# Cross-attention in a decoder layer: key-pair sums on GpSimd, normalisation on ScalarE, the sums' matmuls moved into the middle of a step

## The chip, the cores and the metric

The kernel runs on one core of one Trainium2 chip. The metric is the device time of one execution in microseconds (us); lower is better. The times come from separate timed executions. The profile is one further execution, recorded by the hardware profiler. Engines: PE is TensorE (PEld its weight loads), DVE is VectorE, ACT is ScalarE, POOL is GpSimd, SP is the engine whose queue issues the DMAs.

## What is computed

Inputs are x and ctx, both 16 x 256 x 512 in float32. Three blocks follow one another, each added to x:

```python
x = x + self_attention(layernorm(x))                 # 16 heads, causal, rotary
x = x + cross_attention(layernorm(x), ctx, ctx, gamma)
x = x + expert_mix(layernorm(x))                     # router, top-k tokens per expert

def cross_attention(q, k, v, gamma):                 # all (16, 256, 512)
    h = 8
    qh = q.reshape(16, h, 256 // h, 512)             # heads split the 256 rows: 32 rows each
    kh, vh = (t.reshape(16, h, 256 // h, 512) for t in (k, v))
    qk = einsum('bhdq,bhdl->bhql', qh, kh) / sqrt(32)
    ret = einsum('bhql,bhdl->bhdq', softmax(qk, -1), vh)
    return gamma * ret.reshape(16, 256, 512)
```

So in the cross-attention the contraction runs over 32 rows, and queries and keys are the 512 columns. Only this block is changed.

## The kernel before

The blocks run one after another, with all engines meeting between them: layer norm 1 (to 106 us), self-attention (to about 2014 us), cross-attention (about 2017 to 2704 us), expert mix (the rest).

**Tiles and steps.** The cross-attention has 32 tiles of 128 rows, and a tile holds 4 heads of 32 rows. A tile has 4 steps, one for each chunk `c` of 128 keys, so there are 128 steps `s = 4n + c`. "Step 0" to "step 3" of a tile below mean `c`. In a step PE does, for each of the 4 heads, one `scores` matmul (L774) for the tile that is six steps ahead (AHEAD = 6) and one `transposed_scores` matmul (L783) for this step. After the second head it does the `middle` of the step. At the step's end it does `weigh` (L794, values times weights) and `sums` (L804, a column of ones times weights) for the step before. `weigh` and `sums` are 4 fp32 matmuls each on 32-column strips of the array, shown as 8 instructions each.

**Two passes over the scores.** `scores` exist only to find the maximum of each query: DVE reduces each bank (L941, `xnmx`). A tile's 16 maxima are transposed by PE (`max_transposes`, L819, middle of step 2 for tile n+1), rounded by ACT (`max_round`, L902, `xmhi`), the rest of the rounding is taken by DVE (`max_rest`, L946, `xmlo`), and the two parts are written by DMA as two more rows of the stacked queries (`max_rows`, L736). `transposed_scores` then give scores less maximum, and ACT takes the exponential from PSUM into `xprt` (L878). Scores use two PSUM banks (`xsc`), transposed scores two (`xst`).

**Preparing a tile.** `load` (L711, L712) brings x and ctx, DVE normalises (`normed`, L932, `xn`), ACT rounds to the PE's fast format (`q_round` L867, `k_round` L872), POOL takes the rest (`split`, L752 and L755). The parts are written to DRAM (`write_parts`, L716 and L718) and read back in six DMAs into three sets of stacks of 96 rows (`read_stacks`, L729 and L730). All DMAs are issued by SP, in this order, each `wait_ge` holding up all that is behind it:

```python
for n in range(-4, TILES):
    if tile(n + 2): read_stacks(n + 2)   # waits until both write_parts(n + 2) have landed
    if tile(n + 1): max_rows(n + 1)      # waits for xmhi, then for xmlo
    if tile(n + 3): write_parts(n + 3)
    if tile(n + 4): load(n + 4)
```

The first `scores` that need the stacks of tile n+2 are those of step 4n+2, that is of step 2 of tile n.

**Finishing a tile.** ACT moves the sums out (`sums_evac`, L896), PE brings them to queries on partitions (`sums_by_query`, L826), DVE inverts them (`one_over_sums`, L952), ACT repeats each 32 times (`repeat`, L907), PE transposes back (`inverses`, L834), DVE multiplies (`output`, L956) and adds gamma times the result to x (`residual`, L960), and takes the statistics for the next layer norm (L965, L969). The tables `WORK` say behind which head of which step ACT and DVE do these things, and for which tile.

Of the kernel before, what the change touches and what calls it, by code (L numbers as in the profile page):

```python
# [625 lines left out]
def cross_attention(nc, x1, ctx_in, gamma, sq, sk, mv2, mv3, x2, cst):  # L626
# [4 lines left out]
    with ctx:  # L631
# [16 lines left out]
        gam = sb("gam", [P, 1], F32)  # L648
        tmp = sb("rs_tmp2", [P, 2, TILES], F32)
        rstd = sb("rstd2", [P, TILES], F32)  # L650
        cin = sb("cin", [P, 4, D], F32)
        xn = sb("xn2", [P, D], F32)
        qp = sb("qp", [P, 2, D], F32R)
# [19 lines left out]
        SU = pb("xsu")  # L673
        VB = pb("xvb")

        s_gam, s_var, s_sqrt, s_step = sem("x_gam"), sem("x_var"), sem("x_sqrt"), sem("x_step")
        s_xi = [sem(f"x_xi{i}") for i in range(4)]
        s_ci = [sem(f"x_ci{i}") for i in range(4)]
# [7 lines left out]
        s_mt, s_mhi, s_mlo = sem("x_mt"), sem("x_mhi"), sem("x_mlo")  # L686
        s_vt, s_vte = sem("x_vt"), sem("x_vte")
        s_ts, s_exp = sem("x_ts"), sem("x_exp")
        s_pv, s_su = sem("x_pv"), sem("x_su")
        s_oe, s_se = sem("x_oe"), sem("x_se")  # L690
        s_sq, s_ri, s_rr, s_rt = sem("x_sq"), sem("x_ri"), sem("x_rr"), sem("x_rt")
        s_on, s_x2, s_bn = sem("x_on"), sem("x_x2"), sem("x_bn")
# [2 lines left out]
        cv = ctx_in.rearrange("b (t p) d -> (b t) p d", p=P)  # L695
        x1v = x1.rearrange("b p t d -> b t p d")

        FIRST, LAST = -4 * CB, CB * (TILES + 2)

        def tile(n):  # L700
            return 0 <= n < TILES
# [1 line left out]
        @block.sync  # L703
        def _(sp):
            sp.dma_start(gam[:, :], gamma.rearrange("(a b) -> a b", a=1).broadcast_to([P, 1])).then_inc(s_gam, 16)

            def load(m):
                if m >= 4:
                    sp.wait_ge(s_vt, m - 3)
                    sp.wait_ge(s_klo, m - 3)  # L710
                sp.dma_start(x2[:, m, :], x1v[m // 2, m % 2]).then_inc(s_xi[m % 4], 16)  # L711
                sp.dma_start(cin[:, m % 4, :], cv[m]).then_inc(s_ci[m % 4], 16)  # L712

            def write_parts(m):
                sp.wait_ge(s_qlo, m + 1)
                sp.dma_start(sq[m % 2].rearrange("h p d -> p h d"), qp[:, :, :].bitcast(F32)).then_inc(s_qw, 16)  # L716
                sp.wait_ge(s_klo, m + 1)
                sp.dma_start(sk[m % 2].rearrange("h p d -> p h d"), kp[:, :, :].bitcast(F32)).then_inc(s_kw, 16)  # L718

            def read_stacks(m):  # L720
                sp.wait_ge(s_qw, 16 * m + 16)
                sp.wait_ge(s_kw, 16 * m + 16)
                if m >= STACKS:
                    sp.wait_ge(s_ts, 16 * (m - STACKS) + 16)
                qv = sq[m % 2].rearrange("h (j r) d -> h r j d", j=XPT)
                kv = sk[m % 2].rearrange("h (j r) d -> h r j d", j=XPT)
                for c in range(PARTS):
                    rows = slice(XD * c, XD * (c + 1))
                    sp.dma_start(qst[m % STACKS][rows, :, :].bitcast(F32), qv[c // 2]).then_inc(s_st[m % STACKS], 16)  # L729
                    sp.dma_start(kst[m % STACKS][rows, :, :].bitcast(F32), kv[c % 2]).then_inc(s_st[m % STACKS], 16)  # L730

            def max_rows(m):
                for k, (part, here) in enumerate(((mhi, s_mhi), (mlo, s_mlo))):
                    sp.wait_ge(here, m + 1)
                    row = qst[m % STACKS][KS + k:KS + k + 1, :, :].rearrange("o h (q n) -> o (h q) n", n=P)
                    sp.dma_start(row.bitcast(F32), part[:, :].bitcast(F32)).then_inc(s_row[m % STACKS], 16)  # L736

            for n in range(-4, TILES):
                if tile(n + 2):
                    read_stacks(n + 2)  # L740
                if tile(n + 1):
                    max_rows(n + 1)
                if tile(n + 3):
                    write_parts(n + 3)
                if tile(n + 4):
                    load(n + 4)

        @block.gpsimd
        def _(pool):
            def split(m):  # L750
                pool.wait_ge(s_qhi, m + 1)
                nc.gpsimd.tensor_tensor(qp[:, 1, :], xn[:, :], qp[:, 0, :].bitcast(F32),  # L752
                                        ALU.subtract).then_inc(s_qlo, 1)
                pool.wait_ge(s_khi, m + 1)
                nc.gpsimd.tensor_tensor(kp[:, 1, :], cin[:, m % 4, :], kp[:, 0, :].bitcast(F32),  # L755
                                        ALU.subtract).then_inc(s_klo, 1)

            for i in range(STACKS):
                nc.gpsimd.memset(kst[i][KS:KM, :, :].bitcast(F32), 1.0).then_inc(s_ones, 1)
                pool.wait_ge(s_ones, i + 1)  # L760
            nc.gpsimd.memset(ones[:, :], 1.0).then_inc(s_ones, 1)
            for n in range(-3, TILES + 1):
                if tile(n + 3):
                    split(n + 3)

        @block.tensor
        def _(pe):
# [27 lines left out]
                                            start=(c == 0), stop=(c == CB - 1))  # L795
                last.then_inc(s_pv, 1)

            def sums(s):
                n, c = s // CB, s % CB
                if c == 0:  # L800
                    pe.wait_ge(s_se, n)
                for h in range(XPT):
                    rows = slice(XD * h, XD * (h + 1))
                    last = nc.tensor.matmul(SU[rows, :], ones[:, :], prt[s % RING][:, h, :],  # L804
                                            start=(c == 0), stop=(c == CB - 1))
                last.then_inc(s_su, 1)

            def values(n):
# [26 lines left out]
                last.then_inc(s_rt, 1)  # L835

            def middle(n, c):
                if c == 0 and tile(n):
                    values(n)
                if c == 1 and tile(n - 2):  # L840
                    inverses(n - 2)
                if c == 2 and tile(n + 1):
                    max_transposes(n + 1)
                if c == 3 and tile(n - 1):
                    sums_by_query(n - 1)

            pe.wait_ge(s_ones, STACKS + 1)
            for s in range(FIRST, LAST):
                for i in range(XPT):
                    if 0 <= s + AHEAD < STEPS:  # L850
                        scores(s + AHEAD, i)
                    if 0 <= s < STEPS:
                        transposed_scores(s, i)
                    if i == 1:
                        middle(s // CB, s % CB)
                if 0 <= s - 1 < STEPS:
                    weigh(s - 1)
                    sums(s - 1)

        @block.scalar  # L860
        def _(act):
            rstd_of_all(nc, act, None, rstd, tmp, s_var, s_sqrt, s_step, scale=XSCALE)

            def q_round(m):
                act.wait_ge(s_qn, m + 1)
# [8 lines left out]
            def exps(s, h):  # L874
                act.wait_ge(s_ts, 4 * s + h + 1)
                if h == 0 and s >= RING:
                    act.wait_ge(s_su, s - RING + 1)
                nc.scalar.activation(prt[s % RING][:, h, :], ST[h % 2][:, :], ACT.Exp).then_inc(s_exp, 1)  # L878

            def v_evac(n):  # L880
# [10 lines left out]
                nc.scalar.activation(osb[n % 2][:, :], OB[:, :], ACT.Copy).then_inc(s_oe, 1)  # L891

            def sums_evac(n):
                act.wait_ge(s_su, CB * n + CB)
                act.wait_ge(s_sq, n)
                nc.scalar.activation(ssb[:, :], SU[:, :], ACT.Copy).then_inc(s_se, 1)  # L896

# [6 lines left out]
            def repeat(n):  # L904
                act.wait_ge(s_ri, n + 1)
                act.wait_ge(s_rt, n)
                nc.scalar.activation(rrep[:, :, :].rearrange("p q (h r) -> p (q h) r", r=XD),  # L907
                                     rq[:, :].unsqueeze(2).broadcast_to([P, CB * XPT, XD]), ACT.Copy).then_inc(s_rr, 1)

            WORK = {(0, 1): ((repeat, -2),), (0, 2): ((v_evac, 0),), (1, 0): ((output_evac, -1), (sums_evac, -1)),  # L910
                    (1, 2): ((q_round, 3),), (1, 3): ((k_round, 3),), (2, 2): ((max_round, 1),)}

            for s in range(FIRST, LAST):
                n, c = s // CB, s % CB
# [8 lines left out]
        def _(dve):  # L923
            nc.vector.tensor_scalar(tmp[:, 0, :], mv2[:, :, 1], EPS, None, ALU.add).then_inc(s_var, 1)
            dve.wait_ge(s_var, 1)
            rstd_of_all(nc, None, dve, rstd[:, :], tmp, s_var, s_sqrt, s_step, scale=XSCALE)
            dve.wait_ge(s_gam, 16)

            def normed(m):
                dve.wait_ge(s_xi[m % 4], 16 * (m // 4 + 1))  # L930
                dve.wait_ge(s_qlo, m)
                nc.vector.tensor_scalar(xn[:, :], x2[:, m, :], mv2[:, m, 0:1], rstd[:, m:m + 1],  # L932
                                        ALU.subtract, ALU.mult).then_inc(s_qn, 1)

            def maximum(g, q):
                m, h = g // CB, g % CB
# [16 lines left out]

            def output(n):
                dve.wait_ge(s_rt, n + 1)
                nc.vector.tensor_tensor(onm[:, :], osb[n % 2][:, :], VB[:, :], ALU.mult).then_inc(s_on, 1)  # L956

            def residual(n):
                dve.wait_ge(s_on, n + 1)
                nc.vector.scalar_tensor_tensor(x2[:, n, :], onm[:, :], gam[:, 0:1], x2[:, n, :], ALU.mult,  # L960
                                               ALU.add).then_inc(s_x2, 1)

            def statistics(n):
                dve.wait_ge(s_x2, n + 1)
                nc.vector.bn_stats(bn[:, :], x2[:, n, :]).then_inc(s_bn, 1)  # L965

            def mean_and_variance(n):
                dve.wait_ge(s_bn, 2 * n + 1)
                nc.vector.bn_aggr(mv3[:, n, :], bn[:, :]).then_inc(s_bn, 1)  # L969

            WORK = {(0, 0): ((normed, 3),), (2, 0): ((output, -2),), (2, 1): ((residual, -2),), (2, 2): ((max_rest, 1),),
                    (3, 0): ((statistics, -2),), (3, 1): ((mean_and_variance, -2),), (3, 3): ((one_over_sums, -1),)}

            for s in range(FIRST, LAST):
                n, c = s // CB, s % CB
# [410 lines left out]
```

## Time and profile before

| | before |
|---|---|
| median of 3 timed runs | 3007.75 us (3007.65 to 3009.14) |
| the profiled execution, its own time | 3004.79 us |
| its span in the trace | 3002.7 us |
| PE busy over the span | 2765.7 us (92%) |
| PEld | 2064.0 us (69%) |
| DVE | 1828.5 us (61%) |
| ACT | 1010.2 us (34%) |
| POOL | 589.9 us (20%) |
| mean granted PE clock | 0.962 |

The times of views are from the span's start. "Busy" of an engine is the time in which it has an instruction under way; matmuls are pipelined, so a busy PE need not be at its peak. In the cross-attention the page's slices show PE at 9 tenths, ACT at 5, DVE at 6, POOL at 1 and the DMA engines at 5 to 6. In rows of the order of time, a row is: start, duration, engine, line, operation, out<-in, shapes, count, and in brackets how long the engine was idle before it and what ended that. "issue" means that nothing in the profile was waited for. SPq rows are DMAs being issued by SP. The granted clock of 1.00 is 2.4 GHz, 0.50 is 1.2 GHz.

### The profile page before, as it was taken

The page shows a single profiled execution, that of the slowest core. Times are in us where ns is not written, and L with a number is a line of the kernel's source. Part 1 is how long each engine was busy: PE and PEld are TensorE (multiplying, and loading weights), DVE is VectorE, ACT ScalarE, POOL GpSimd, SP SyncE. Part 2 cuts the span into 40 slices and gives each one's busy share as a digit, 9 for nine tenths or more (in the row PEclk, how much of TensorE's full clock was granted, in tenths as well). Part 3 has the DMA queues.
Part 4 walks back from the last instruction along what each step waited for, and adds up shares of the span by engine and source line. Part 5 has one row for each costly group of instructions (what it writes and reads, how often), then busy time and mean ns, then how long its engine had stood idle before and what let it go on. Part 6 is the DMA issues. An engine that isn't in the chain of part 4 may idle for free. (4 is left out here: it accounts for less than half of the span.)

```text
span 3002.7 us, 40644 instructions
## 1 busy us (share of the span) xinstructions
PE 2765.7 (92%) x14237; PEld 2064.0 (69%) x14238; DVE 1828.5 (61%) x3578; ACT 1010.2 (34%) x2511; POOL 589.9 (20%) x498
## 2 busy tenths in 40 slices
PE   3799999999999999999999999977999999997973
PEld 2588888888888888888888888863444444447852
DVE  7465556566656665565656566655666666643488
ACT  2222222322222332222322222223555555553321
POOL 2121112321211321111322111211111111100263
PEclk9999999999999999999999999997999999995697
DMA  8421122222211421221222112117666556610003
GB/s 315 154 84 57 57 92 92 85 71 99 71 57 57 154 71 57 73 96 57 92 90 101 57 57 99 43 55 186 152 164 166 155 149 165 164 42 18 0 0 112
DMA packets 165203, 290.02 MB, mean 97 GB/s; under 512 B 11680, under 2 KB 78240, under 8 KB 162976
## 3 DMA queue, kind: packets, MB, share of 16 engines
q1 hardware_dynamic: 165024, 287.66, 30.9%
q8 instruction: 110, 1.80, 0.3%
q14 instruction: 69, 0.57, 0.1%
HBM read 194.81 MB, written 92.27 MB: 96 GB/s over the span
## 5 line engine op out<-in xcount | busy, mean ns | idle before, releaser
L439 PE MATMUL pj<-xnt,whi 128*128 128x512 f32 x2048 | 704.1, 405 | 16.1 <-DMA xnt<-xt_scratch 16.1
L519 ACT ACTIVATE pr<-sc,nmx 128x128 f32<-128x128 f32 (+1 forms) x512 | 210.6, 416 | 934.0 <-DVE nmx L591 934.0
L941 DVE TENSOR_REDUCE xnmx<-xsc 128x1 f32<-128x512 f32 x512 | 338.6, 683 | 231.2 <-PE xsc L774 228.2
L439 PEld LDWEIGHTS pj<-xnt,whi 128*128 128x128 f32 x2048 | 385.6, 188 | 108.3 <-DMA xnt<-xt_scratch 16.5
L439 PE MATMUL pj<-xnt,wlo 128*128 128x512 f32 x1024 | 398.6, 389 | 0.0
L394 POOL TENSOR_TENSOR qt<-rot,swp 128x512 f32<-128x512 f32 x128 | 166.0, 1297 | 1126.4 <-DVE swp L572 1126.4
L878 ACT ACTIVATE xprt<-xst 128x512 f32<-128x512 f32 x512 | 294.0, 603 | 264.2 <-PE xst L783 262.4
L436 PE MATMUL pj<-whi,xnt 128*128 128x512 f32 x1024 | 351.7, 405 | 0.0
L570 DVE TENSOR_TENSOR rot<-pj,trig 128x512 f32<-128x512 f32 x256 | 176.8, 691 | 226.6 <-PE pj L439 226.6
L774 PE MATMUL xsc<-kst,qst 96*128 96x512 f32 x512 | 245.1, 483 | 52.5 <-DMA kst<-sk_scratch 29.9
L591 DVE TENSOR_REDUCE nmx<-sc 128x1 f32<-128x128 f32 (+1 forms) x512 | 158.3, 351 | 177.4 <-PE sc L465 172.8
L600 DVE TENSOR_SCALAR pr<-pr,rinv 128x128 f32<-128x128 f32 (+1 forms) x512 | 251.8, 533 | 9.0
L774 PEld LDWEIGHTS xsc<-kst,qst 96*128 96x128 f32 x512 | 98.8, 193 | 224.5 <-DVE xnmx L941 111.5
L436 PEld LDWEIGHTS pj<-whi,xnt 128*128 128x128 f32 x1024 | 192.5, 188 | 45.9
L783 PE MATMUL xst<-qst,kst 98*128 98x512 f32 x512 | 207.6, 408 | 17.1 <-ACT xprt L878 17.1
L394 POOL TENSOR_TENSOR kt<-rot,swp 128x512 f32<-128x512 f32 x128 | 165.0, 1289 | 296.4 <-DVE swp L572 296.4
L439 PEld LDWEIGHTS pj<-xnt,wlo 128*128 128x128 f32 x1024 | 193.9, 189 | 34.5
L452 PE MATMUL pj<-whi,ohi 128*128 128x512 f32 x512 | 212.5, 415 | 1.4 <-DVE olo L605 1.4
L579 DVE TENSOR_TENSOR xio<-pj,xio 128x512 f32<-128x512 f32 x128 | 88.5, 691 | 192.3 <-PE pj L452 192.3
L452 PE MATMUL pj<-whi,olo 128*128 128x512 f32 x512 | 201.6, 394 | 0.0
L452 PE MATMUL pj<-wlo,ohi 128*128 128x512 f32 x512 | 199.1, 389 | 0.0
L436 PE MATMUL pj<-wlo,xnt 128*128 128x512 f32 x512 | 199.1, 389 | 0.0
(152 smaller groups left out, 4483.4 us busy)
## 6 DMA issues: line engine op xcount, KB each, us to landing
xnt<-xt_scratch SPq DMA_DIRECT2D x64, 1024.0 KB, 8.0
x_scratch<-xio SPq DMA_DIRECT2D x64, 512.0 KB, 3.6
xio<-x_scratch SPq DMA_DIRECT2D x48, 512.0 KB, 4.1
qst<-sq_scratch SPq DMA_DIRECT2D x96, 256.0 KB, 5.6
kst<-sk_scratch SPq DMA_DIRECT2D x96, 256.0 KB, 6.2
xt_scratch<-parts SPq DMA_DIRECT2D x16, 1024.0 KB, 4.7
sq_scratch<-qp SPq DMA_DIRECT2D x32, 512.0 KB, 3.0
sk_scratch<-kp SPq DMA_DIRECT2D x32, 512.0 KB, 4.1
```

Of the source, the lines that this page charges most:

```text
L394: nc.gpsimd.tensor_tensor(qk["QK".index(kind)][h][:, :, :].rearrange("p b n -> p (b n)"), rot[r % 2][:, :], swp[r % 2][:, :], ALU.add).the ...
L436: last = nc.tensor.matmul(bank[:, :], moving[:, i * P:(i + 1) * P], wpart[:, w, :], start=(k == 0), stop=(k == 3 * CB - 1))
L439: last = nc.tensor.matmul(bank[:, :], wpart[:, w, i * HD:(i + 1) * HD], moving, start=(k == 0), stop=(k == 3 * CB - 1))
L452: last = nc.tensor.matmul(PJ[n % 3][:, :], o[:, h, tok], w[:, CH_O + h, :], start=(h == 0 and k == 0), stop=(h == HG - 1 and k == 2))
L519: nc.scalar.activation(pr[:, a % 4, lo:hi], SC[a % 2][:, lo:hi], ACT.Exp, bias=nmx[:, a % 4, t:t + 1], accum_out=rsum[:, a % 4, t:t + 1]). ...
L570: nc.vector.tensor_tensor(ro, bank, table(slice(0, P), q), ALU.mult)
L591: nc.vector.tensor_reduce(nmx[:, a % 4, t:t + 1], SC[a % 2][:, lo:hi], AX.X, ALU.max, negate=True).then_inc(s_nmx, 1)
L600: nc.vector.tensor_scalar(pr[:, a % 4, lo:hi], pr[:, a % 4, lo:hi], rinv[:, a % 4, t:t + 1], None, ALU.mult).then_inc(s_pr, 1)
L774: nc.tensor.matmul(SC[q % 2][:, :], qst[m % STACKS][0:KS, h, q * P:(q + 1) * P], kst[m % STACKS][0:KS, h, :], start=True, stop=True).then_ ...
L783: nc.tensor.matmul(ST[h % 2][:, :], kst[n % STACKS][0:KM, h, c * P:(c + 1) * P], qst[n % STACKS][0:KM, h, :], start=True, stop=True).then_ ...
L878: nc.scalar.activation(prt[s % RING][:, h, :], ST[h % 2][:, :], ACT.Exp).then_inc(s_exp, 1)
L941: nc.vector.tensor_reduce(nmx[:, m % 2, k:k + 1], SC[q % 2][:, :], AX.X, ALU.max, negate=True).then_inc(s_mx, 1)
```

## The change

- **Pair sums on POOL.** For each pair of neighbouring steps POOL adds the weights of the second to those of the first, in place, in 4 pieces of 128x512 (`pair_sum`). PE then multiplies by ones only once for a pair: 2 groups of `sums` in a tile in place of 4.
- **Where the sums' groups are.** They are no longer at a step's end but in its middle: for tile n-1, in steps 0 and 2, before the values' transposes and before the maxima's transposes.
- **Normalisation on ACT.** `normed` leaves DVE (step 0, head 0) and is one activation on ACT (step 0, head 3) with scale `rstd` and bias `shift` = -mean x rstd, which one new DVE instruction makes for all tiles.
- **Residual on POOL.** gamma is multiplied in `repeat`; the addition to x is a 128x512 addition on POOL. The statistics on DVE follow one tile later (steps 0 of tile n for tile n-3).
- **ACT's order.** `sums_evac` moves from step 1, head 0 to step 2, head 3; `q_round` and `k_round` one head earlier.
- **SP's order.** The first four `load`s are issued ahead of everything; in the steady loop the order is as it was. The loops of the steps run 3 steps longer.

```diff
-        FIRST, LAST = -4 * CB, CB * (TILES + 2)
+        FIRST, LAST = -4 * CB, CB * (TILES + 2) + 3
@@ block.sync
-            for n in range(-4, TILES):
+            for m in range(4):
+                load(m)
+            for n in range(-3, TILES):
...
-                if tile(n + 4):
+                if n >= 0 and tile(n + 4):
                     load(n + 4)
@@ block.gpsimd
+            def pair_sum(n, k):
+                s = CB * n + 2 * k
+                a, b = prt[s % RING], prt[(s + 1) % RING]
+                pool.wait_ge(s_pv, s + 1)
+                for h in range(XPT):
+                    pool.wait_ge(s_exp, 4 * (s + 1) + h + 1)
+                    nc.gpsimd.tensor_tensor(a[:, h, :], a[:, h, :], b[:, h, :], ALU.add).then_inc(s_add, 1)
+
+            def residual(n):
+                pool.wait_ge(s_on, n + 1)
+                nc.gpsimd.tensor_tensor(x2[:, n, :], onm[:, :], x2[:, n, :], ALU.add).then_inc(s_x2, 1)
...
-            for n in range(-3, TILES + 1):
+            for n in range(-3, TILES + 2):
+                if tile(n - 1):
+                    pair_sum(n - 1, 1)
                 if tile(n + 3):
                     split(n + 3)
+                if tile(n):
+                    pair_sum(n, 0)
+                if tile(n - 2):
+                    residual(n - 2)
@@ block.tensor
-            def sums(s):
-                n, c = s // CB, s % CB
-                if c == 0:
+            def sums(n, k):
+                pe.wait_ge(s_add, XPT * (2 * n + k + 1))
+                if k == 0:
                     pe.wait_ge(s_se, n)
...
             def middle(n, c):
-                if c == 0 and tile(n):
-                    values(n)
+                if c == 0:
+                    if tile(n - 1):
+                        sums(n - 1, 0)
+                    if tile(n):
+                        values(n)
                 if c == 1 and tile(n - 2):
                     inverses(n - 2)
-                if c == 2 and tile(n + 1):
-                    max_transposes(n + 1)
+                if c == 2:
+                    if tile(n - 1):
+                        sums(n - 1, 1)
+                    if tile(n + 1):
+                        max_transposes(n + 1)
...
                     weigh(s - 1)
-                    sums(s - 1)
@@ block.scalar
+            def normed(m):
+                act.wait_ge(s_xi[m % 4], 16 * (m // 4 + 1))
+                act.wait_ge(s_qlo, m)
+                nc.scalar.activation(xn[:, :], x2[:, m, :], ACT.Identity, scale=rstd[:, m:m + 1],
+                                     bias=shift[:, m:m + 1]).then_inc(s_qn, 1)
...
-            WORK = {(0, 1): ((repeat, -2),), (0, 2): ((v_evac, 0),), (1, 0): ((output_evac, -1), (sums_evac, -1)),
-                    (1, 2): ((q_round, 3),), (1, 3): ((k_round, 3),), (2, 2): ((max_round, 1),)}
+            WORK = {(0, 1): ((repeat, -2),), (0, 2): ((v_evac, 0),), (0, 3): ((normed, 3),), (1, 0): ((output_evac, -1),), (1, 1): ((q_round, 3),),
+                    (1, 2): ((k_round, 3),), (2, 2): ((max_round, 1),), (2, 3): ((sums_evac, -1),)}
@@ block.vector
-            WORK = {(0, 0): ((normed, 3),), (2, 0): ((output, -2),), (2, 1): ((residual, -2),), (2, 2): ((max_rest, 1),),
-                    (3, 0): ((statistics, -2),), (3, 1): ((mean_and_variance, -2),), (3, 3): ((one_over_sums, -1),)}
+            WORK = {(0, 1): ((statistics, -3),), (0, 2): ((mean_and_variance, -3),), (2, 0): ((output, -2),),
+                    (2, 2): ((max_rest, 1),), (3, 3): ((one_over_sums, -1),)}
```

The exponentials' wait for a free buffer of the ring of 5 changes with it: a buffer that was added to waits for the pair's `sums`, one that was added from for POOL's additions.

## Rows read from the trace of the kernel before

**Rows 1.** Order of time, PE's weight loads: one tile's step starts and step ends.

```profile
2300.61 0.19 PEld L774 LDWEIGHTS xsc<-kst,qst 96*128 96x128 f32 x1 [0.84 <-issue]
...
2303.60 0.16 PEld L794 LDWEIGHTS xob<-xprt,vt 128*32 128x32 f32 x8 [0.36 <-ACT xprt L878]
2304.06 0.13 PEld L804 LDWEIGHTS xsu<-xprt,xones 128*32 128x32 f32 x4 [0.30 <-issue]
2304.49 0.13 PEld L804 LDWEIGHTS xsu<-xprt,xones 128*32 128x32 f32 x4 [0.30 <-issue]
2305.46 0.19 PEld L774 LDWEIGHTS xsc<-kst,qst 96*128 96x128 f32 x1 [0.84 <-issue]
...
2308.35 0.19 PEld L783 LDWEIGHTS xst<-qst,kst 98*128 98x128 f32 x1 [0.82 <-ACT xprt L878]
...
2310.74 0.19 PEld L774 LDWEIGHTS xsc<-kst,qst 96*128 96x128 f32 x1 [0.94 <-DMA kst<-sk_scratch]
...
2313.22 0.19 PEld L774 LDWEIGHTS xsc<-kst,qst 96*128 96x128 f32 x1 [0.86 <-DVE xnmx L941]
...
2315.74 0.19 PEld L774 LDWEIGHTS xsc<-kst,qst 96*128 96x128 f32 x1 [0.84 <-DVE xnmx L941]
...
2320.73 0.19 PEld L774 LDWEIGHTS xsc<-kst,qst 96*128 96x128 f32 x1 [0.84 <-issue]
```

**Rows 2.** Waits, SP's own, 2100 to 2650 us: total us, times, longest.

```profile
SPq L736 <- ACT xmhi L902: 279.3, 27, 10.9
SPq L724 <- DMA sk_scratch<-kp: 47.3, 28, 3.3
```

**Rows 3.** Order of time, step 2 of the tile of rows 1, then SP's queue.

```profile
2312.02 0.50 PE L774 MATMUL xsc<-kst,qst 96*128 96x512 f32 x1
...
2312.80 0.60 ACT L878 ACTIVATE xprt<-xst 128x512 f32<-128x512 f32 x1 [0.20 <-PE xst L783]
...
2313.29 0.25 ACT L902 ACTIVATE xmhi<-xmx 16x128 fp32r<-16x128 f32 x1
...
2314.34 0.27 DVE L946 TENSOR_TENSOR xmlo<-xmx,xmhi 16x128 fp32r<-16x128 f32 x1
...
2314.64 0.51 SPq L736 DMA_DIRECT2D qst<-xmlo  x1
...
2322.59 0.43 SPq L730 DMA_DIRECT2D kst<-sk_scratch  x1
```

**Rows 4.** Issue to landing of the one kst read issued at 2322.59.

```profile
DMA to landing us min/median/max: 7.1/7.1/7.1
```

**Rows 5.** Order of time, first and last step 2 that wait for a read of stacks.

```profile
2070.63 0.50 PE L774 MATMUL xsc<-kst,qst 96*128 96x512 f32 x1 [2.02 <-DMA kst<-sk_scratch]
...
2650.78 0.19 PEld L774 LDWEIGHTS xsc<-kst,qst 96*128 96x128 f32 x1 [0.84 <-DMA kst<-sk_scratch]
```

**Rows 6.** Groups by line, 2050 to 2750 us: the costs of a POOL piece and of DVE's residual.

```profile
L755 POOL TENSOR_TENSOR kp<-cin,kp 128x512 fp32r<-128x512 f32 x30 | 38.5, 1285 | 0.0
...
L960 DVE SCALAR_TENSOR_TENSOR x<-xonm,gam,x 128x512 f32<-128x512 f32 x32 | 23.8, 743 | 0.1
```

**Rows 7.** Order of time: ctx's second load at the start, the block's last instruction.

```profile
2027.09 0.95 SPq L712 DMA_DIRECT2D cin<-in_ctx_in_dram  x1
...
2704.15 0.18 DVE L969 BATCH_NORM_AGGREGATE mv<-bn 128x2 f32<-128x6 f32 x1
```

**Rows 8.** Busy time and granted clock (third last column), after the stall before 2070.63.

```profile
2072.00:2073.00 1.00, 1.00 (x4) 0.54 (x4) 1.00 (x2) 0.81 (x2) 0.00 (x0) 0.87 0.00 0
...
2075.00:2076.00 1.00, 1.00 (x8) 0.20 (x4) 0.00 (x0) 0.00 (x0) 0.00 (x0) 0.50 0.15 53
2076.00:2077.00 1.00, 1.00 (x10) 0.32 (x3) 0.00 (x0) 0.00 (x0) 0.00 (x0) 0.92 1.01 379
```

**Rows 9.** Order of time, a stall in the self-attention.

```profile
1520.73 0.67 PE L484 MATMUL ob<-prt,v 128*128 128x256 f32 x2 [2.06 <-DVE olo L605]
```

**Rows 10.** Busy time and granted clock behind the stall of rows 9.

```profile
1522.00:1524.00 2.00, 2.00 (x10) 1.61 (x9) 1.92 (x5) 0.45 (x2) 0.80 (x1) 1.00 0.88 315
```

More of the change, by code:

```diff
@@ L650, in cross_attention @@
         rstd = sb("rstd2", [P, TILES], F32)
+        shift = sb("shift2", [P, TILES], F32)
         cin = sb("cin", [P, 4, D], F32)
@@ L674, in cross_attention @@
         VB = pb("xvb")
+        s_shift = sem("x_shift")
         s_gam, s_var, s_sqrt, s_step = sem("x_gam"), sem("x_var"), sem("x_sqrt"), sem("x_step")
@@ L688, in cross_attention @@
         s_ts, s_exp = sem("x_ts"), sem("x_exp")
-        s_pv, s_su = sem("x_pv"), sem("x_su")
+        s_pv, s_add, s_su = sem("x_pv"), sem("x_add"), sem("x_su")
         s_oe, s_se = sem("x_oe"), sem("x_se")
@@ L803, in sums @@
                     rows = slice(XD * h, XD * (h + 1))
-                    last = nc.tensor.matmul(SU[rows, :], ones[:, :], prt[s % RING][:, h, :],
-                                            start=(c == 0), stop=(c == CB - 1))
+                    last = nc.tensor.matmul(SU[rows, :], ones[:, :], prt[(CB * n + 2 * k) % RING][:, h, :],
+                                            start=(k == 0), stop=(k == 1))
                 last.then_inc(s_su, 1)
@@ L862, in _ @@
             rstd_of_all(nc, act, None, rstd, tmp, s_var, s_sqrt, s_step, scale=XSCALE)
+            act.wait_ge(s_gam, 16)
+            act.wait_ge(s_shift, 1)
+            def normed(m):
[3 more added lines that the diff above has]
+                                     bias=shift[:, m:m + 1]).then_inc(s_qn, 1)
             def q_round(m):
@@ L876, in exps @@
                 if h == 0 and s >= RING:
-                    act.wait_ge(s_su, s - RING + 1)
+                    old = s - RING
+                    act.wait_ge(s_pv, old + 1)
+                    if old % 2 == 0:
+                        act.wait_ge(s_su, old // 2 + 1)
+                    else:
+                        act.wait_ge(s_add, XPT * (old // 2 + 1))
                 nc.scalar.activation(prt[s % RING][:, h, :], ST[h % 2][:, :], ACT.Exp).then_inc(s_exp, 1)
@@ L893, in sums_evac @@
             def sums_evac(n):
-                act.wait_ge(s_su, CB * n + CB)
+                act.wait_ge(s_su, 2 * n + 2)
                 act.wait_ge(s_sq, n)
@@ L907, in repeat @@
                 nc.scalar.activation(rrep[:, :, :].rearrange("p q (h r) -> p (q h) r", r=XD),
-                                     rq[:, :].unsqueeze(2).broadcast_to([P, CB * XPT, XD]), ACT.Copy).then_inc(s_rr, 1)
-            WORK = {(0, 1): ((repeat, -2),), (0, 2): ((v_evac, 0),), (1, 0): ((output_evac, -1), (sums_evac, -1)),
-                    (1, 2): ((q_round, 3),), (1, 3): ((k_round, 3),), (2, 2): ((max_round, 1),)}
+                                     rq[:, :].unsqueeze(2).broadcast_to([P, CB * XPT, XD]), ACT.Copy,
+                                     scale=gam[:, 0:1]).then_inc(s_rr, 1)
+            WORK = {(0, 1): ((repeat, -2),), (0, 2): ((v_evac, 0),), (0, 3): ((normed, 3),), (1, 0): ((output_evac, -1),), (1, 1): ((q_round, 3),),
+                    (1, 2): ((k_round, 3),), (2, 2): ((max_round, 1),), (2, 3): ((sums_evac, -1),)}
             for s in range(FIRST, LAST):
@@ L926, in _ @@
             rstd_of_all(nc, None, dve, rstd[:, :], tmp, s_var, s_sqrt, s_step, scale=XSCALE)
[L927 to L933, printed above, removed]
+            nc.vector.scalar_tensor_tensor(shift[:, :], mv2[:, :, 0], -1.0, rstd[:, :], ALU.mult, ALU.mult).then_inc(s_shift, 1)
             def maximum(g, q):
@@ L955, in output @@
                 dve.wait_ge(s_rt, n + 1)
+                dve.wait_ge(s_x2, n)
                 nc.vector.tensor_tensor(onm[:, :], osb[n % 2][:, :], VB[:, :], ALU.mult).then_inc(s_on, 1)
[L958 to L961, printed above, removed]
             def statistics(n):
                 dve.wait_ge(s_x2, n + 1)
+                dve.wait_ge(s_bn, 2 * n)
                 nc.vector.bn_stats(bn[:, :], x2[:, n, :]).then_inc(s_bn, 1)
```

## Prediction

> **What bounds the kernel now.** I read the order of time of PE's weight loads first, to cut a tile into its four steps. A tile takes 20.1 us [rows 1]: steps of 4.85, 5.28, 5.00 and 4.99 us. A step ends with `weigh` and `sums`, together 1.86 us (2303.60 to 2305.46), of which a group of `sums` is two passes 0.43 us apart, 0.87 us. What the change takes away thus stands on PE's path, and PE looks like the bound. The reader should then look at the start of step 2. At 2310.74 the weight load was ended by a DMA, the last read of the key stacks, with 0.94 us of idle time where 0.84 us is what such a load always shows. So PE and the DMAs are within 0.1 us of one another there.
>
> The second view is SP's own waits. SP waited 279 us in 27 tiles, some 10 us a tile, for `xmhi` [rows 2]. All that SP does behind that wait is late with it: the row of `xmlo`, then both `write_parts`, two loads, then `read_stacks`, which also waits until the writes have landed (47 us in 28 tiles). The reads land for PE's step 2, and `xmhi` is made from transposes in PE's step 2. That closes a ring, one turn per tile, and PE's other work isn't in it:
>
> scores of step 2 start, maxima transposed, rounded, rest taken, row of `xmlo` issued, parts written, stacks read, scores of the next tile's step 2.
>
> Its length [rows 3, 4]: from 2310.74 to the issue of `xmlo`'s row at 2314.64 is 3.90 us; from there to the last issue of a read, 2322.59, 7.95 us; to its landing 7.1 us. The queue's part is 15.05 us in that tile. Over the 30 tiles whose reads are waited for it is 14.7 to 16.2 us, mean 15.44. The ring is 3.90 + 15.44 + 0.03 = 19.4 us on average, and up to 20.1 us. The tile's mean is (2650.78 - 2070.63) / 29 = 20.0 us [rows 5]. So PE's path is the longer, by 0.6 us on average, and in the tiles with late reads by nothing. **Whatever is taken off PE's path beyond 0.6 us a tile is not gained unless the ring gets shorter too.**
>
> **The change, part by part.** *PE's own path.* Two groups of `sums` fewer: 2 x 0.87 = 1.7 us. A group in the middle of a step has to drain and refill the array beside full-height matmuls; no row shows that. Bounds: 0.87 us, as at the step's end, and 1.2 us (the 0.87 with one more wait of 0.30 us as in rows 1); I take 1.05, nearer to what the end of a step shows with its neighbours. In step 1 the wait of 0.82 us for ACT (2308.35) goes, since `sums_evac` leaves that place; in step 2 most of the 0.86 us for DVE (2313.22) goes, with `residual`. New steps: 4.85 - 0.87 + 1.05 - 0.3 = 4.7; 5.28 - 0.87 - 0.6 = 3.8; 5.00 - 0.87 + 1.05 - 0.7 = 4.5; 4.99 - 0.87 = 4.1; together 17.1 us. If PE alone set the time the change would bring 2.9 us a tile.
>
> *POOL* gets 8 pieces and a residual at 1.285 us [rows 6]: with its two of `split`, 11 x 1.285 = 14.1 us a tile. That is below 17.1. Its order also holds: the additions of pair 1 start at step 0 and end 5.2 us later, before step 2 needs them and before `q_round` releases `split` in step 1; those of pair 0 follow in step 2 and are wanted in the next tile. `write_parts` waits for `split`, but only after `xmlo`'s row, some 5 us later. *DVE* loses 0.74 us [rows 6] and `normed`; *ACT* gains `normed`, about 0.6 us like its other 128x512 pieces [rows 3], hidden behind PE in step 0. The Trainium skill's page "SBUF — State Buffer", section "SBUF: two separate sides", says that VectorE with two SBUF inputs and GpSimd lock one another out; only DVE's `residual` had two such inputs here, and it leaves, so I add nothing for contention. No row of before has POOL busy all the time beside DVE and shows this.
>
> *The ring.* In SP's steady order nothing changes, so the 15.44 us stay: no DMA is removed, and each waits for the same things. But step 2 is where the second group of `sums` now stands, **ahead of the transposes of the maxima**. Before: third scores at 1.28 us after the step's start, its exponential at 2.06, `xmhi` at 2.55 to 2.80, `xmlo` at 3.60 to 3.87, its row issued at 3.90 [rows 1, 3]. After: the transposes 1.05 us later, third scores at 2.3, exponential at 3.1 and, behind it on ACT, `xmhi` 3.6 to 3.85. `xmlo` no longer waits for `residual` and follows at 4.1; but its row is issued behind that of `xmhi` (3.88, and 0.51 us each with a gap), at 4.44. So the ring gets **0.54 us longer**, to 4.44 + 15.44 + 0.03 = 19.9 us. Bounds for this term: +0.2 (a group of 0.87 and the row of `xmhi` no hindrance) and +0.8.
>
> *The stall and the clock.* With PE's work at 17.1 us and the ring at 19.9, PE stands still for 2.8 us before every step 2. Before, it did so once, for 2.02 us before 2070.63 [rows 5]. Behind that the granted clock fell in 2072 to 2073 and was 0.50 until 2076 [rows 8], that is 1.2 GHz for some 3.4 us, with the PE busy again. Against it: a stall of 2.06 us in the self-attention [rows 9], with the clock at 1.00 behind it [rows 10]. The new stalls are longer than both and come in each tile, with a thin step 1 before them, so I take it that the clock falls in most tiles, within 2 us after the stall. Its price is what of the ring is PE's work: from the step's start to the third transposed scores, 2.65 us, which at half clock takes twice as long. A low stretch that covers all of it costs up to 1.7 us (half of 3.4), one that begins 2 us in costs 0.7; none costs 0. I take 1.1. The other low time is PE's own and falls into the stall.
>
> The page "TensorE: Matmul & The Clock Gate" of the Trainium skill, section "HAM oscillation — how this bites in real kernels", tells of a kernel whose PE waits for a DMA in every tile and starts each one at the low clock. By it my forecast is the 21.0 us below; its waits are longer than those here, so it doesn't settle it, and rows 8 agree with it where rows 9 and 10 don't.
>
> *Start and end.* At the start the loads of tiles 1 to 3 no longer stand between the writes and the reads of tile 0 (2027.09 [rows 7]), and `normed` of tile 1 waits for less: 2 us less (bounds 0.5 and 3). At the end, from 2650.78 to 2704.33 [rows 5, 7], no read is waited for: the last ten steps lose about 4.5 us (of their groups of `sums` half, 0.87 each, less what ACT then holds up). After the last `weigh` but one, POOL's four additions, 5.1 us, replace `sums` and `weigh` that ran there, and the last residual costs 0.54 us more: +4. Net 0, give or take 3.
>
> **Sum.** A tile: 4.44 + 1.1 + 15.44 + 0.03 = 21.0 us against 20.0; 29 tiles: +29 us. Start -2, end 0: +27 us. The profiled execution took 3004.79 us (span 3002.7), 3.0 us under the median of the runs; from it 3032, and from the median, against which I predict, **3035 us**. Own range: price of the clock 0.7 to 1.7, 3023 to 3052.
>
> **Rivals.** *The clock stays up.* Tile 19.9 us, 29 x -0.1 = -3, start -2: 3003 us, with the ring's bounds of +0.2 and +0.8 2993 to 3011. For it: rows 9 and 10. Against: rows 8, at a shorter stall. The work saved shows as PE's idle time, no gain.
> *The ring gets shorter.* The reads land at their fastest, 14.7 us in each tile, as DMAs meet less work of their own kind: 4.44 + 14.7 + 0.03 = 19.2 us, 29 x -0.8 - 2 = -26: 2982 us. For it only that some tiles before show it; against it that the same bytes go in the same order.
> *PE was the bound all along* (the ring isn't one): 17.1 + 0.3 for chance waits, 29 x -2.6 = -75, 2931 us. Against it: the waits of rows 2 and the landing at 2310.7.
> *Low clock for longer*, two stretches after each stall, or a slower POOL (14.1 us leaves room up to 1.9 us a piece): the ring at 22 us or more, 3063 us.
> That the change doesn't do what it says I can't find: the 1024 instructions of `sums` must become 512.
>
> **Chances.** Forecast 0.55, clock stays up 0.26, shorter ring 0.08, PE the bound 0.04, longer still 0.07. The range takes the forecast's 3023 to 3052, the gap and most of the second case: 2998 to 3052. A measurement of this kernel tells 0.2%, 6 us, from no change. Slower by more (over 3014): nearly all of the forecast, the last case and none of the others, 0.60. Same (3002 to 3014): half or more of the second case and a corner of the first, 0.19. Faster: 0.21.
>
> **What would show it.** PE's weight loads: `xsc` of step 2 waiting 2 us or more for `kst<-sk_scratch` in each tile, and a tile of 21.0 us. The row of `xmlo` issued 4.4 us after the step's start at full clock, 5.5 on average. The granted clock in steady tiles down to 0.50 behind the stall, 0.92 or so on the mean. POOL busy 14 us a tile. Wrong if: no stall there; stalls with the clock at 1.00; a queue's part other than 15.4 us; or SP waiting for `split`.

## The result and the profile after

The changed kernel took **3038.44 us** (median of 4 runs, 3035.5 to 3044.58) against 3007.7 us before: ratio 1.0106, 95% interval 1.0093 to 1.0118. It is slower by 1.1%, or 31 us. The forecast was 3035.

The profiled execution took 3037.34 us. From its page, the span, the busy time of each engine, and the slices of PE and of the granted clock (PEclk):

```profile
span 3035.6 us, 40037 instructions
...
PE 2755.8 (91%) x13725; PEld 2063.6 (68%) x13726; DVE 1798.1 (59%) x3515; ACT 1033.3 (34%) x2543; POOL 946.3 (31%) x786
...
PE   3799999999999999999999999958888888887973
...
PEclk9999999999999999999999999977998989995597
```

PE does 10 us less than before and POOL 356 us more, and over the whole span both kernels have PE at 9 tenths. Nothing in these sums says why the kernel is slower. The slices point at it: in the cross-attention those of PE show 8 where they showed 9, and those of the clock now show 8s.

The cross-attention's busy times and clock (third last column), before and then after:

```profile
2300.00:2400.00 100.00, 94.00 (x569) 44.42 (x565) 64.33 (x115) 59.18 (x115) 12.64 (x10) 1.00 0.61 160
```

```profile
2300.00:2400.00 100.00, 87.55 (x457) 41.76 (x456) 56.74 (x99) 58.99 (x114) 63.31 (x52) 0.90 0.58 148
```

PE went from 94% busy to 88% at a mean clock of 0.90, and the DMAs moved less in the same time. Where PE's time went stands in the waits of 2100 to 2650 us, those of PE for DMAs, and SP's own:

```profile
PE xsc L796 <- DMA kst<-sk_scratch: 69.4, 26, 3.7
```

```profile
SPq L738 <- ACT xmhi L942: 316.3, 26, 13.3
SPq L726 <- DMA sk_scratch<-kp: 40.9, 25, 2.6
```

In every one of these 26 tiles PE stands still before step 2, 2.7 us on average (69.4 / 26), for the last read of the stacks. SP, which issues the reads, waits 12 us a tile for `xmhi`, where it was 10 [rows 2]. It doesn't wait for `split` at all.

One step 2 in which the clock stayed up, in order of time (the answer to rows 3):

```profile
2410.32 0.50 PE L796 MATMUL xsc<-kst,qst 96*128 96x512 f32 x1 [1.96 <-DMA kst<-sk_scratch]
...
2411.44 1.07 PE L826 MATMUL xsu<-xprt,xones 128*32 128x512 f32 x8
...
2412.44 0.28 PE L841 MATMUL xmx<-ident,xnmx 128*16 128x128 f32 x1
...
2413.22 0.60 ACT L918 ACTIVATE xprt<-xst 128x512 f32<-128x512 f32 x1 [1.05 <-PE xst L805]
...
2413.72 0.25 ACT L942 ACTIVATE xmhi<-xmx 16x128 fp32r<-16x128 f32 x1
...
2414.55 0.59 SPq L738 DMA_DIRECT2D qst<-xmlo  x1
```

The group of sums (L826) runs at 1.1 us after the step's start, the transposes of the maxima (L841) only at 2.1, and the row of `xmlo` is issued at 4.23 us; before it was 3.90. And one in which the clock fell:

```profile
2306.30 0.70 PE L796 MATMUL xsc<-kst,qst 96*128 96x512 f32 x1 [3.03 <-DMA kst<-sk_scratch]
...
2308.21 1.85 PE L826 MATMUL xsu<-xprt,xones 128*32 128x512 f32 x8
...
2312.09 0.59 SPq L738 DMA_DIRECT2D qst<-xmlo  x1
```

```profile
2307.00:2310.00 3.00, 3.00 (x12) 0.68 (x12) 1.89 (x3) 1.19 (x2) 3.00 (x4) 0.53 0.00 0
```

Here PE had stood still 3.03 us, the granted clock of 2307 to 2310 was 0.53, the group took 1.85 us in place of 1.07, and the row came 5.79 us after the step's start. Of the 29 tiles between the first and the last such wait, 3 had 4.23 us, the others 4.5 to 6.5, the mean is 5.74. These 3, in which the clock stayed at 1.00, had the shortest stalls before them (1.65, 1.93 and 1.96 us); the other 26 had 1.99 to 3.73 us. From there to the last landing it took 15.43 us on average, and 0.04 us more to the start of the scores. 5.74 + 15.43 + 0.04 = 21.2 us, and the tile was (2685.92 - 2070.85) / 29 = 21.2 us.

Against the trace of before, the span is 32.9 us longer. From the block's first instruction to the first wait for a read it is 2.1 us less (51.4 against 53.5). The 29 tiles: +34.9 us. From there to the block's last instruction: -2.6 us. Outside of the cross-attention, in code that didn't change, +2.6 us, of which 2.3 lie ahead of it; the block began between 2017.0 and 2023.0 us in the kernels below.

### The profile page after: what moved, and what is told of

Same layout as the page of the kernel before. It is cut to its first block and busy times, and to the rows that moved or that the text cites. A ratio compares the mean times of both kernels' runs of the same rounds, so it can differ in the third digit from the quotient of the medians.

```text
span 3035.6 us, 40037 instructions
## 1 busy us (share of the span) xinstructions
PE 2755.8 (91%) x13725; PEld 2063.6 (68%) x13726; DVE 1798.1 (59%) x3515; ACT 1033.3 (34%) x2543; POOL 946.3 (31%) x786
## 5 line engine op out<-in xcount | busy, mean ns | idle before, releaser
L768 POOL TENSOR_TENSOR xprt<-xprt 128x512 f32<-128x512 f32 x256 | 319.0, 1278 | 165.6 <-PE xob L816 165.6
L796 PE MATMUL xsc<-kst,qst 96*128 96x512 f32 x512 | 253.5, 499 | 106.3 <-DMA kst<-sk_scratch 104.2
L796 PEld LDWEIGHTS xsc<-kst,qst 96*128 96x128 f32 x512 | 108.3, 212 | 241.8 <-DMA kst<-sk_scratch 105.1
L805 PE MATMUL xst<-qst,kst 98*128 98x512 f32 x512 | 223.4, 439 | 2.4 <-ACT xprt L918 0.9
```

The source lines that it names most:

```text
L768: nc.gpsimd.tensor_tensor(a[:, h, :], a[:, h, :], b[:, h, :], ALU.add).then_inc(s_add, 1)
L796: nc.tensor.matmul(SC[q % 2][:, :], qst[m % STACKS][0:KS, h, q * P:(q + 1) * P], kst[m % STACKS][0:KS, h, :], start=True, stop=True).then_ ...
L805: nc.tensor.matmul(ST[h % 2][:, :], kst[n % STACKS][0:KM, h, c * P:(c + 1) * P], qst[n % STACKS][0:KM, h, :], start=True, stop=True).then_ ...
```

## The experiments

"The tile" is from here on the time between the issues of `xmlo`'s row, mean of 27 tiles of a kernel's one profile: 20.04 us before, 21.28 after. Ratios are to the kernel before on the same chip. The edits are to the changed kernel where nothing else is said.

| kernel | median us | ratio (95%) | tile us | clock, 2100 to 2550 us |
|---|---|---|---|---|
| sums before the stall | 3003.82 | 0.999 (0.9975 to 1.0004) | 19.95 | 0.91 |
| writes first | 2917.78 | 0.9699 (0.9683 to 0.9716) | 17.14 | 1.00 |
| filler in the stall | 2998.89 | 0.9973 (0.9963 to 0.9982) | 19.99 | 0.99 |
| before, half of the sums | 2989.68 | 0.9939 (0.9922 to 0.9955) | 19.62 | 0.98 |
| before, writes first | 3002.99 | 0.9983 (0.9974 to 0.9992) | 19.98 | 1.00 |
| sums before the stall, writes first | 2926.66 | 0.9728 (0.9713 to 0.9743) | 17.43 | 1.00 |
| the same, rows last | 2925.67 | 0.9725 (0.971 to 0.974) | 17.38 | 1.00 |
| sums before the stall, filler | 2980.79 | 0.9913 (0.9898 to 0.9928) | 19.14 | 0.99 |
| transposes first | 2950.19 | 0.9811 (0.9794 to 0.9827) | 18.33 | 0.98 |
| writes first, four stacks | 2914.57 | 0.9696 (0.968 to 0.9712) | 16.96 | 1.00 |

**Does the ring hold the tile? The writes ahead of the rows of the maxima.**

```diff
-                if tile(n + 1):
-                    max_rows(n + 1)
                 if tile(n + 3):
                     write_parts(n + 3)
+                if tile(n + 1):
+                    max_rows(n + 1)
```

> The changed kernel, but SP issues the two writes of tile n+3 ahead of the maxima's rows of tile n+1 (two calls swapped in SP's loop, nothing else). My theory: the ring is cut, since the writes no longer stand behind xmhi and xmlo; PE's own 17.1 to 17.5 us a tile remain, the stall before step 2 falls under 0.5 us and the granted clock stays at 1.00: 29 x (17.4 - 21.2) = -110, 2928 us (range 2915 to 2950). Rival A (DMA bandwidth: the DMA engines are busy 0.6 of the time and the reads would only land later after their issue): tile still 19 us or more, 2975 us or more. Rival B (POOL's pieces set the tile): 3038 us.

Measured 2917.78 us, tile 17.14, clock 1.00: 120 us less than the changed kernel from two calls that change places. No engine does anything else, so neither POOL's pieces nor PE's work nor the bytes of the DMAs held the changed kernel. SP's waits in 2100 to 2600 us:

```profile
SPq L718 <- POOL qp L756: 183.7, 27, 7.1
SPq L738 <- ACT xmhi L942: 79.7, 29, 14.7
SPq L726 <- PE xst L805: 38.6, 27, 2.5
```

The wait for `xmhi` fell from 12 us a tile to under 3; SP now waits for `split`, which isn't late, and for PE to free the stacks.

**Is the low clock a cause or only a sign? More work in the stall.**

```diff
                     weigh(s - 1)
+                if s % CB == 1 and tile(s // CB) and tile(s // CB + 2):
+                    for i in range(10):
+                        nc.tensor.matmul(MX[:, P:D], k[0:KS, 0, 0:P], q[0:KS, 0, P:D], start=True, stop=True)
```

(Written here in one piece; `k` and `q` are the stacks of the tile, and nobody reads the result.)

> The changed kernel with 10 extra matmuls (96 rows, 384 columns, their result isn't used) behind weigh at the end of step 1 of tiles 0 to 29, that is in PE's stall. They add work and shorten nothing. My theory (the low clock after the stall makes PE's part of the ring longer): the granted clock stays at 1.00, the row of xmlo comes 4.2 us after step 2's start in every tile, the tile is 4.2 + 15.4 + 0.05 = 19.7 us: 29 x -1.5 = -43, 2995 us (range 2985 to 3010): faster by adding work. Rival (the low clock costs nothing, since it falls into PE's spare time): 3038 us. Rival (the fillers are too long for the stall): 3045 us or more.

Measured 2998.89 us, 39.6 us less than the changed kernel, by 300 matmuls more. The row of `xmlo` came 4.25 us after the step's start in most tiles; the queue's part, 15.5 us, was what it had been. The busy times and the clock:

```profile
2100.00:2550.00 450.00, 425.07 (x2418) 224.84 (x2415) 270.01 (x471) 280.21 (x542) 311.07 (x250) 0.99 0.63 160
```

So the low clock cost 1.3 us a tile (21.28 - 19.99), for PE's part of the ring is made longer by it.

**Is it the place of the group? The second group of sums at the end of step 1.**

```diff
                 if c == 2:
-                    if tile(n - 1):
-                        sums(n - 1, 1)
...
                     weigh(s - 1)
+                if s % CB == 1 and tile(s // CB - 1):
+                    sums(s // CB - 1, 1)
```

> The changed kernel, but the second group of sums of tile n-1 stands at the end of step 1 (where PE waits for the reads anyway) and no longer in step 2 ahead of the transposes of the maxima. Same instructions, same count, another place. My theory (the ring from step 2 over xmlo, writes and reads to the next step 2 sets the tile): the row of xmlo is issued about 3.4 us after the step's start at full clock in place of 4.2, the tile is 3.4 + 15.4 + 0.05 = 18.9 us if the clock stays up and 19.6 if it still falls in part of the tiles, in place of 21.2: 2971 to 2992 us, likeliest 2980. Rival A (PE's or POOL's total work sets the tile): no total changes, 3038 us. Rival B (the group costs the same wherever it is): 3038 us.

Measured 3003.82 us: 35 us less, so the place counts, but 24 us more than I expected and outside my range. The row of `xmlo` did come 3.36 to 3.39 us after the step's start in 24 of 29 tiles. But before 8 of 30 steps 2 PE didn't wait for a read at all; it was late itself. One of them, busy times and clock:

```profile
2184.00:2188.00 4.00, 3.84 (x13) 1.96 (x17) 3.02 (x6) 1.93 (x5) 4.00 (x4) 0.69 0.00 0
2188.00:2192.00 4.00, 4.00 (x15) 1.98 (x8) 1.69 (x3) 1.81 (x4) 1.37 (x2) 0.50 0.59 219
2192.00:2196.00 4.00, 4.00 (x18) 2.43 (x18) 1.58 (x4) 1.55 (x3) 0.00 (x0) 0.50 0.60 179
2196.00:2200.00 4.00, 4.00 (x20) 1.37 (x12) 1.99 (x3) 1.55 (x3) 2.88 (x3) 0.61 0.99 201
```

PE itself had stood still 1.64 us before 2184.16. The clock then stayed at 0.50 for over 10 us with PE busy in all of them, and the next step 2 started 23.1 us after this one. The freeing of the stacks was then late as well, which is a wait of SP that the changed kernel had once (2100 to 2650 us):

```profile
SPq L726 <- PE xst L805: 36.5, 11, 5.9
```

**Is that what was missing? The same with a filler.** Five of the filler's matmuls behind the group.

> The changed kernel with the second group of sums at the end of step 1 (which gave 3004 us where I expected 2980, a tile of 20.0 us with the clock low for up to 13.7 us at a time while PE was busy) and 5 extra matmuls of 96 rows and 384 columns behind it, in what is left of the stall. They only add work. My theory for the miss (the long low stretches made PE's own path 20 us or more in a third of the tiles; the ring itself is 18.9 us): with the clock held at 1.00 the tile is 3.4 + 15.4 + 0.05 = 18.9 us, 29 x -1.1 = -32, 2972 us (range 2962 to 2985). Rival (the reads themselves got slower, or POOL held the tile): 3004 us or more.

Measured 2980.79 us, tile 19.14, clock 0.99. 23 us came back with more work on PE, and the tile is within 0.3 us of the ring's 18.9. The miss was the low clock on PE's own path.

**Was there a ring in the kernel before? Half of its sums left out.** To the kernel before:

```diff
+                if c >= 2:
+                    nc.tensor.matmul(SU[0:XD, 0:8], ones[:, :], prt[s % RING][:, 0, 0:8],
+                                     start=True, stop=True).then_inc(s_su, 1)
+                    return
```

> The kernel before, with the sums' groups of steps 2 and 3 of a tile left out (one matmul of 8 columns stands in for each, so the denominators are those of half of the keys and the output is not the reference's). Takes 1.7 us of PE's work from a tile without touching anything of the ring, DVE, POOL or ACT. My theory: PE then waits at step 2 for the reads, tile = 3.90 + 15.44 + 0.05 = 19.4 us, 29 x -0.6 = -17, at the end -4: 2987 us. Rival (PE alone set the time of the kernel before): 20.0 - 1.7 = 18.3 us, 29 x -1.7 = -50, at the end -4: 2954 us.

This kernel leaves out the sums over half of the keys and is there for its time alone. Measured 2989.68 us, tile 19.62: of 1.7 us of PE's work taken away, 0.4 us came through. The two steps that lost a group did get 0.8 us shorter each (medians, 5.00 to 4.16 and 4.86 to 4.03 us). PE's waits in 2100 to 2550 us:

```profile
PE xsc L774 <- DMA kst<-sk_scratch: 16.3, 18, 1.2
```

Some 0.7 us a tile stands here, as a wait for the same read: PE's idle time in step 1 went from 0.5 to 1.2 us. Another 0.4 us is in step 2, whose mean went from 5.00 to 5.44 us with its median still at 5.00, since the clock fell after some of these waits (0.98 on the mean). This is what the change ran into, with POOL, ACT and DVE as they were.

**What would cutting the ring have brought before the change?** The two calls swapped in the kernel before.

> The kernel before (nothing of the change), with only SP's two calls swapped: the writes of tile n+3 ahead of the maxima's rows of tile n+1. The ring is cut, but PE's own 20.0 us a tile remain. My theory (PE's path was the longer by 0.6 us, the ring mattered only in the tiles with late reads): tile 20.0 us, 3005 to 3008 us, no change. Rival (the ring held the kernel before too, PE's work alone is shorter): below 2995 us. With the same swap in the changed kernel giving 2918 us this says what the change is worth once the ring is cut.

Measured 3002.99 us, ratio 0.9983 (0.9974 to 0.9992): 5 us, less than the 0.2% that I called no change but clear of it, and between my range and the rival's. In the profile the block is 4.8 us shorter. Of this 2.7 us lie before the first step 2 that needs a read and 1.6 us in the tile behind it: there the kernel before had waited 2.02 us and then had the low clock [rows 5, 8], and this one did neither. Two tiles with late reads went from 20.12 and 20.11 us to 20.04 and 20.02; the others are the same within 0.05 us. So in the steady tiles the ring held those with late reads and no others, as the prediction had it, and most of the 5 us was at the start. With the ring cut in both, the change brings 3002.99 to 2917.78 us: 85 us, 2.8%.

**What bounds the kernel once the ring is cut?** Three kernels. First, both edits together:

> The changed kernel with both edits: second group of sums at the end of step 1, and the writes ahead of the maxima's rows. With the writes ahead alone a tile took 17.1 us and PE still waited 0.4 us for the reads before step 2. The group of 1 us at the end of step 1 fills that wait. PE's work sets the tile: 16.7 to 16.9 us, 29 x -0.3 = -9, 2909 us (range 2900 to 2918). Rival (the reads, held up now by the transposed scores that still use the stacks, bound the tile in the same way wherever the group is): 2918 us.

Measured 2926.66 us: slower than with the writes first alone, and outside the range that I gave. The steps tell it (medians): step 1 went from 4.22 to 4.72 us, step 2 only from 4.27 to 4.14. In the middle of step 2 the group costs PE 0.13 us net. About half of its 1.0 us falls into a wait for DVE, which is back in this kernel, where the group has gone:

```profile
2314.84 0.51 PE L796 MATMUL xsc<-kst,qst 96*128 96x512 f32 x1 [0.47 <-DVE xnmx L975]
```

(In the kernel before PE waited as long at this place, 0.46 us before 2313.22; the 0.86 us of [rows 1] are the weight load's.) Where the rest goes I didn't follow. At the end of step 1 the group costs its full time, less the wait of 0.4 us that it fills. So for PE the middle of step 2 was the cheaper place. Second, the loads ahead of the rows too:

> As the kernel with both edits, and the loads of tile n+4 ahead of the maxima's rows as well, which come last in SP's loop. With the writes ahead alone the reads were held up 1.4 us a tile by PE's transposed scores, not by the rows of the maxima: so the rows' place no longer matters, and the time is that of the kernel with both edits, 2909 us (within 5 us). Rival (the rows' wait still delays the reads): 5 to 10 us faster than that.

Measured 2925.67 us: no difference, as expected of the order; the level is that of the kernel above and shares its miss. Third, writes first and four stacks (`STACKS = 4`):

> The changed kernel with the writes ahead of the maxima's rows (2918 us) and four sets of stacks in place of three. There SP waited 1.4 us a tile for PE's transposed scores to free the stacks before it issued the reads, and PE 0.4 us for the reads. My theory: both waits go, PE's work of 16.7 us sets the tile: 29 x -0.4 = -12, 2906 us (range 2898 to 2914). Rival (the DMAs' bandwidth sets when the reads land): 2918 us.

Measured 2914.57 us, ratio 0.9696 (0.968 to 0.9712) beside 0.9699 (0.9683 to 0.9716): the two can't be told apart, and my 2906 us (at most 2914) wasn't reached. SP's wait for PE's transposed scores is gone from the answer, and the tile of the profile is 0.2 us shorter, but PE still waits 0.2 us a tile for reads (5.0 us in 27 tiles). What sets those last tenths I didn't follow further.

**Can the group stay where it is, with SP's order as it was?** Transposes first, and the rounding one head earlier.

```diff
                 if c == 2:
-                    if tile(n - 1):
-                        sums(n - 1, 1)
                     if tile(n + 1):
                         max_transposes(n + 1)
+                    if tile(n - 1):
+                        sums(n - 1, 1)
...
-                    (2, 2): ((max_round, 1),)
+                    (2, 1): ((max_round, 1),)
...
-                    (2, 2): ((max_rest, 1),)
+                    (2, 1): ((max_rest, 1),)
```

> The changed kernel, SP's order as it is there, but in the middle of step 2 the transposes of the maxima come before the group of sums, and the rounding on ACT and the rest on DVE one head earlier. The group stays in the middle of the step. My theory: the row of xmlo is issued 2.8 us after the step's start (4.2 at full clock in the changed kernel), ring 2.8 + 15.4 + 0.05 = 18.3 us; PE needs 16.7 us; a stall of 1.5 us or more stays, so the clock still falls in part of the tiles, 18.3 to 19.5 us a tile: 29 x -2.3 = -67, 2972 us (range 2950 to 2995). Rival (the group costs PE the same and the order within the step is of no account): 3038 us.

Measured 2950.19 us, tile 18.33, clock 0.98: 88 us less than the changed kernel from the order of two calls in the middle of a step and one head on two engines, at the low end of my range since the clock fell in few tiles (8 of 29). PE still waits 1.05 us a tile for the reads (26.3 us in 25 tiles).

## Why the prediction was right, step by step

- **The ring, not PE's path, sets the tile: shown.** Writes first takes 120 us off with no work moved; half of the sums taken from the kernel before brings 0.4 us of 1.7, and PE waits longer for the same read.
- **The queue's part stays 15.4 us: right.** 15.4 on average after (15.43 over the 29 turns).
- **The ring longer by 0.54 us at full clock: right in kind, too much in size.** The row came at 4.23 us, +0.33, inside the bounds of 0.2 and 0.8. I had the exponential of the third head at 3.1 us and `xmhi` at 3.6; they came at 2.90 and 3.40, since the group costs 1.0 us there and the third scores follow the transposes without a gap. The row of `xmlo` did go out right behind that of `xmhi`, 0.56 us later.
- **The clock falls in most tiles: right; its price of 1.1 us: too small.** 26 of 29 tiles, 1.51 us on average (5.74 - 4.23), and 1.3 by the filler. In 10 tiles the row came at 6.47 us, 2.24 us late: I had taken half of the 3.4 us of rows 8 as the most, but low stretches twice as long occur. The clock's mean was 0.90, where I had 0.92. In the kernel with the sums before the stall, low stretches were longer still; that was my last rival, and I had given it the low clock's longer price only on the ring. On PE's own path it costs as much.
- **PE's own work of 17.1 us a tile: 0.4 too high.** With the writes first the tile is 17.1 us, of which 0.4 is a wait for reads. Without that wait the steps are 4.6, 3.8, 4.3 and 4.0 us, where I had 4.7, 3.8, 4.5 and 4.1. In step 2 I had the new group less the wait for DVE at +0.35 us (1.05 - 0.7), and it is +0.13. In step 3 the group that left took 1.05 us with it and not 0.87. I had also taken the idle times of the weight loads in [rows 1], 0.82 and 0.86 us, for PE's, which are 0.51 and 0.46 at these places. The forecast didn't rest on this term, because the ring was the longer.
- **POOL busy 14 us a tile and not in the way: right.** 322.5 us in 500, 13.7 a tile; the pieces took 1278 ns beside 1285 [rows 6]. No piece got longer beside DVE, and DVE had no operation with two SBUF inputs left. By the rule of the Trainium skill's page "SBUF — State Buffer", section "SBUF: two separate sides", there was nothing to lock; the rows agree (the longest of the 256 pieces took 1298 ns), but no run here tests the lock itself.
- **`normed` on ACT at 0.6 us: 0.82 us,** hidden all the same.
- **Start -2 us: -2.1. End 0: -2.6,** inside the 3 us either way.
- The two sizes missed, -0.2 at full clock and +0.4 for the clock, nearly cancel: 21.0 forecast, 21.2 measured. That the time came within 3 us is luck in part. The tiles were 6 us more than forecast, the end -3, code outside of the block +3, and the median stood 1.1 us over the profiled execution where I had taken 3.0.

## What to carry to other kernels

Before work is taken off the busiest engine, look for a ring: a wait for a DMA whose source goes back, over a queue in order, to the same engine's same step one turn earlier. Where such a ring is as long as the engine's own path, the work saved becomes a stall, and what counts is what stands inside the ring: here an order of two calls was worth more than the whole change, and the change was worth 2.8% only behind it. Change and swap together are 3.0% faster than the kernel before (2917.78 us, or 2914.57 with a fourth set of stacks).
A stall of one to three us that comes in every turn isn't free time on TensorE: look at the granted clock behind it.

## What was not expected of the hardware

- In the kernel with the sums before the stall the clock fell after PE's stalls of 1.1 to 1.8 us too, shorter than the 2.02 us of [rows 5] and the 2.06 us of [rows 9], behind which it stayed up. It was then at 1.2 GHz for 10 to 13.7 us at a time with PE busy nearly all the while (seven such stretches in 500 us), where the kernel before had 3.4 us. In the changed kernel the stretches were 3.4 or 6.8 us. So the length of the stall alone doesn't settle it; what does stays open.
- 300 matmuls that nobody needs made the changed kernel 1.3% faster.
